# The normalised image turned between the two convolutions, and three steps beside it put later

## The reference

```python
x = x + L0(_gn(x))      # pixel similarity: s = relu(cos(p, q)) ** 2 over all pairs of pixels, y = s @ (W x + b)
x = x + L1(_gn(x))      # deformable convolution
# L1:
offset = conv2d_same(conv2d_same(x, w1, b1), w2, b2)     # 3x3, 128 -> 128 -> 72 channels
return relu(deform_conv(x, offset, wd))                  # 3x3, 4 groups: bilinear samples at shifted positions
```

## Time and profile before

| | |
|---|---|
| time, median of 3 runs | 460.2 us (459.57 to 460.83) |
| the profiled execution | 459.05 us, its span 457.0 us |
| busy: TensorE | 405.2 us (89%) |
| busy: VectorE, ScalarE, GpSimd | 339.5 us (74%), 215.6 us (47%), 90.0 us (20%) |
| mean granted TensorE clock | 0.970 |
| all DMA queues | 32.71 MB, mean 72 GB/s |
| stages 0, 1, 2, 3 (TensorE) | about 108 to 217, 217 to 319, 319 to 402, 402 to 457 us |

### The profile page before, as it was taken

How to read it: one execution, slowest core, us unless ns; L and a number is a source line. 1 busy time by engine, 2 the same in 40 slices (tenths; PEclk the granted TensorE clock), 3 DMA queues, 4 the chain that set the end, 5 groups by cost and what they waited for, 6 DMA issues and landing times.

```text
span 457.0 us, 9689 instructions
## 1 busy us (share of the span) xinstructions
PE 405.2 (89%) x3887; PEld 291.9 (64%) x3887; DVE 339.5 (74%) x586; ACT 215.6 (47%) x392; POOL 90.0 (20%) x99
## 2 busy tenths in 40 slices
PE   6698989979998789799999798989869898979996
PEld 6455557646665565678666575768556566857875
DVE  5995776829999999388854999376979945779901
ACT  3343254345555365441655446331845643257661
POOL 5444470001774100000546100000010000000000
PEclk9899999999999899999999899989979997999999
DMA  7200002250011124332001313442213243303330
GB/s 252 77 0 0 0 2 75 84 141 1 2 47 46 47 67 146 85 90 91 12 13 36 92 54 94 124 126 81 59 47 100 90 122 98 104 23 107 96 105 24
DMA packets 46157, 32.71 MB, mean 72 GB/s; under 512 B 3264, under 2 KB 43488, under 8 KB 46112
## 3 DMA queue, kind: packets, MB, share of 16 engines
q1 hardware_dynamic: 46048, 31.95, 23.5%
q10 hardware_dynamic: 64, 0.13, 0.1%
HBM read 25.24 MB, written 10.37 MB: 78 GB/s over the span
## 4 chain that ended last, share of the span: by engine, by line
PE 46%; DVE 32%; DMA 6%; SPq 5%; issue 4%; ACT 4%; POOL 1%; DVEq 0%; ACTq 0%; POOLq 0%
PE psB L788 10%; PE psB L555 9%; PE psT L739 7%; DVE wpix L1507 7%; PE psV L762 5%; DVE combo L1294 4%; PE psA L646 4%; DMA h_scr<-h_ring 3%; SPq L320 3%; DVE combo_p L1298 2%; DVE tent L1488 2%; PE psA L555 2%; DVE tent L1482 2%; PE psB L813 2%; PE psA L813 2%
## 5 line engine op out<-in xcount | busy, mean ns | idle before, releaser
L1021 ACT ACTIVATE wcell<-psT 128x512 f32<-128x512 f32 (+1 forms) x160 | 83.9, 552 | 70.2 <-PE psT L739 68.9
L1507 DVE TENSOR_TENSOR wpix<-tent 128x512 f32<-128x512 f32 (+1 forms) x160 | 99.7, 675 | 14.4 <-PE psT L739 13.3
L739 PE MATMUL psT<-ident,wpix 128*128 128x128 f32 x576 | 89.1, 288 | 12.4 <-ACT wcell L1021 12.0
L739 PEld LDWEIGHTS psT<-ident,wpix 128*128 128x128 f32 x576 | 68.8, 148 | 37.2 <-issue 29.5
L493 POOL TENSOR_TENSOR sim<-rel 128x512 f32<-128x512 f32 x48 | 61.4, 1299 | 69.0 <-ACT rel L978 69.0
L1045 ACT ACTIVATE val<-psV 128x576 f32<-128x576 f32 x64 | 44.0, 688 | 30.7 <-PE psV L762 30.2
L788 PE MATMUL psB<-val,wd_sb 128*128 128x256 f32 x216 | 51.2, 392 | 0.0
L762 PE MATMUL psV<-wcell,hwin 64*32 64x144 f32 x2048 | 47.2, 294 | 3.9 <-ACT val L1045 3.5
L646 PE MATMUL psA<-sim,scratch 128*128 128x512 f32 x96 | 45.6, 597 | 0.6 <-POOL sim L493 0.6
L788 PEld LDWEIGHTS psB<-val,wd_sb 128*128 128x128 f32 x216 | 40.7, 193 | 8.3 <-issue 2.9
L555 PE MATMUL psB<-g_p 128*128 128x512 f32 x144 | 40.9, 419 | 0.0
(11 more groups left out here) (193 smaller groups left out, 453.6 us busy)
## 6 DMA issues: line engine op xcount, KB each, us to landing
hwin<-h_scr SPq DMA_DIRECT2D x128, 128.0 KB, 2.9
h_scr<-h_ring SPq DMA_DIRECT2D x8, 576.0 KB
h_ring<-sim SPq DMA_DIRECT2D x4, 512.0 KB
x_all<-x SPq DMA_DIRECT2D x1, 1536.0 KB, 10.0
out<-yout SPq DMA_DIRECT2D x12, 128.0 KB, 1.8
off_scr<-sim SPq DMA_DIRECT2D x4, 288.0 KB
combo<-sim SPq DMA_DIRECT2D x32, 32.0 KB
val<-w SPq DMA_DIRECT2D x1, 576.0 KB, 6.1
```

What stands on the lines that cost most here:

```text
L739: last = pe.transpose(bank[:, at:at + P], wpix[:, t % 2, k, 2 * h:2 * h + 2, :].rearrange("p g q -> p (g q)"), ident[:, :])
L1021: act.activation(wcell[:, t % 2, taps[0]:taps[-1] + 1, :, :].rearrange("q k h p -> q (k h p)"), bank[:, 0:len(taps) * G // 2 * P], ACT.Cop ...
L1507: dve.tensor_tensor(w, ty, tx, ALU.mult).then_inc(s["weights_done"], 1)
```

## The change

In the steady stages the image is turned in slot 45 instead of 33, between the two convolutions. It now waits for conv1's output rows, and conv2 instead of conv1 waits for the copied image. On SyncE the store comes a tile later, ahead of the windows of tile 6, and the copy into windows ahead of those of tile 7, just ahead of the shifts. The offsets are turned in slots 67 and 69 instead of 65 and 67, with the first weights behind them in slot 69. The fourth batch's square moves from slot 56 to 57, its high and low parts from 58 to 60, the norms, gx and inversion from 61 to 62, add and scale from 62 to 63. The start before stage 0 keeps its slots.

```diff
-                      shift=None, turn={65: (0, 1), 67: (2, 3)}, extremes=70)
-        LEAD_IMAGE, STEADY_IMAGE, IMAGE_TILE = 38, 33, 5
+                      shift=None, turn={67: (0, 1), 69: (2, 3)}, extremes=70)
+        LEAD_IMAGE, STEADY_IMAGE, IMAGE_TILE = 38, 45, 6
...
-        PREP = {56: ("normalise", "square"), 58: ("high", "low"), 61: ("norms", "gx", "invert"), 62: ("add", "scale"),
+        PREP = {56: ("normalise",), 57: ("square",), 60: ("high", "low"), 62: ("norms", "gx", "invert"), 63: ("add", "scale"),
                 71: ("diagonal",)}
...
-        LEAD_WEIGHTS, FIRST_WEIGHTS, LEAD_EXTREMES = 60, 67, 12
+        LEAD_WEIGHTS, FIRST_WEIGHTS, LEAD_EXTREMES = 60, 69, 12
...
                     if t == IMAGE_TILE and b + 1 < B:
                         store_image(b + 1)
-                    if t == IMAGE_TILE + 1 and b + 1 < B:
+                    if t == ROWT - 1 and b + 1 < B:
                         lay_image(b + 1)
...
-                    if kx == 0 and which == 0 and v == 2:
+                    if kx == 0 and v == 2 and which == (1 if b else 0):
                         pe.wait_ge(s["image_copied"], 2 * (b + 1))
...
                 pe.wait_ge(s["flat_done"], b + 1)
                 if b > 0:
-                    pe.wait_ge(s["orelu_done"], 4 * (b - 1) + ORELU0)
-                if b + 1 < B:
-                    pe.wait_ge(s["rel_done"], 2 * QT * (b + 2 if b else 1))
+                    pe.wait_ge(s["conv1_done"], 2 * (b + 1))
+                else:
+                    pe.wait_ge(s["rel_done"], 2 * QT)
```

## The result

The changed kernel takes 464.97 us (median of 4 runs, 464.35 to 466.63) against 460.29 us (459.57 to 460.83) before: a ratio of 1.0108, with a 95% interval of 1.0078 to 1.0139. It is about 4.7 us slower; forecast was no change (460.0, range 456.5 to 463.0). The profiled execution of after took 464.68 us, its span 462.8 us against 457.0, at a mean clock of 0.958 against 0.970.

What follows compares the result with a forecast made beforehand. Chain of waits: TensorE 46%, VectorE 32%, transfers and SyncE's issuing 11%. Terms 0.6 - 3.5 + 2.4 + 0.3 = -0.2 us on 459.05 gave 458.85; with 1.15 us to the median, 460.0 us, range 456.5 to 463.0.

Steps and rivals of the forecast that it cites:

- the fourth batch's gain: Stage 0: ScalarE evicts psT ahead of the square, TensorE gets 2.30 us back; dconv 3.5 us earlier.
- slot 33's 0.2 us each: Image turn out of slot 33: 0 at full clock, 0.2 us each in stages 0, 1, 2 for the clock.
- the landing: Offsets' shifts land behind the copy on SyncE's queue, at 196.0, 301.8 and 383.1 us in stages 0 to 2.
- the stretch between landing and dconv: Offsets landed to dconv going on: 2.4 us in stage 0, 4.0 to 4.3 in stages 1 and 2.
- The two terms: Offsets' landing: 14.0 us for lay_image's copy on four engines, plus 1.7 us for nine shifts queued behind it.
- The halt at slot 60: Stage 0, TensorE waiting for an eviction of psT: down from 2.69 us to 0.4.
- the six matmuls: dconv behind the offsets' halt: 1.56 us at full clock, 2.93 at half; stage 1 may lose 0 to 1.4.
- Slot 45: Image turn into slot 45: 1.0 us of transposes hidden by a halt of 0.86; taken as 0, bounds 0 to 0.3.
- the later turn: Offsets' turn, stages 1 and 2: four transposes now come ahead of it, 0.35 us, twice that at half clock.
- Slower by the clock: Lengthened halts at slots 33 and 67 cost clock too: +3, 463 us; chance 0.28, including without stage 0's gain.
- The shifts don't queue: Stages 1 and 2 halt only 1.5 us at the offsets, -1 each, stage 0 -3.8: 455 us; chance 0.10.
- Faster, as the clock comes back soon: Offsets to dconv 2.4 us and matmuls at full clock in stages 1 and 2: about 457 us; chance 0.20.
- The fourth, that the change does nothing it says: Halt at slot 60 stays, stage 0 gives 0 to -1; ends in the slower case, chance 0.28.

Runs made afterwards that it cites:

- fill67: Changed kernel with 36 transposes of the identity, read by nobody, ahead of the wait for the offsets in stages 1 and 2: 460.25 us.
- copy12: Changed kernel with the copy into windows written rows first, spread over 12 transfer engines instead of 4: 453.56 us.
- image_undone: Changed kernel with the image turned in slot 33 again as before; the fourth batch and offsets keep their new slots: 451.91 us.
- fill33: Changed kernel with 32 transposes of the identity, read by nobody, in TensorE's halt of slot 33 in stages 0 and 1: 465.95 us.
- prep_undone: Changed kernel with the fourth batch's old slots: 467.34 us.
- copy12_fill33: Changed kernel with the copy on 12 engines and 32 unread transposes in the halt of slot 33 of stages 0 and 1: 452.67 us.
- image_only: Kernel before with the image's move alone; the fourth batch and the offsets in their old slots: 468.24 us.
- turn_undone: Changed kernel with the offsets turned in slots 65 and 67 again, the first weights in 67: 468.41 us.
- copy12_turn_undone: Changed kernel with the copy on 12 engines and the offsets turned in slots 65 and 67: 457.87 us.

## Why the prediction was wrong

**The mechanism was right, its sizes weren't.** The forecast had the fourth batch's gain spent on shifts that queue behind the copy. The runs show both. With slot 33's 0.2 us each, stages 0 to 3 were forecast at -3.3, +2.6, +0.5 and 0; they came out at -1.4, +4.3, +1.5 and +1.4.

The step that failed first is the landing: 14.0 us for the copy and 1.7 for the shifts. It took 0.9 to 1.7 us longer in each stage, 3.6 of the some 6 us that the sum was short of. The next is the stretch between landing and dconv in stages 1 and 2, which ran wholly at half clock behind the longer halts (4.59 us, where 4.0 to 4.3 were taken). The rest is mainly the 1.4 us of stage 3, of which the prediction has nothing; what slot 33 was off by in the three stages nearly cancels.

**When the offsets land.** The two terms gave 15.7 us from lay_image's issue to TensorE's turn. It took 16.7, 17.4 and 16.6 us (198.04 behind 181.34 in stage 0, 302.17 behind 284.73 in stage 1, 386.25 behind 369.69 in stage 2). That is 1.0 us more in stage 0, 1.7 in stage 1 and 0.9 in stage 2. The 14.0 us came from a copy that ran alone; here windows and shifts ran beside it. Which of the two terms was short is not shown.

**Stage 0.** The other 1.0 us of its miss came with slot 33: SyncE issued lay_image at 181.34 and not 180.3. Tile 6's windows ahead of it, which wait for a sample, went out 0.89 us later than in before, just as the sample of slot 38 came 0.89 us later. Then 2.5 us from the turn to dconv, reckoned as 2.4. The halt at slot 60 was as forecast (0.39).

**The clock behind the turn.** Between landing and dconv the forecast had 4.0 to 4.3 us in stages 1 and 2, from a row that was itself partly at half clock, and 0.5 of the possible 1.4 us for the six matmuls. Measured were 4.59 us and 1.85 for the matmuls in stage 1. The larger error here is what was not asked: that in the new slots this stretch runs in 2.5 us at full clock, so that the clock alone decides over 2 us in each stage. fill67, copy12 and image_undone each show 2.5. For stage 0 the prediction had summed up just that, 2.4 us; for stages 1 and 2 it took the old slots' row.

**Slot 33.** At full clock 0, as forecast (fill33: the sample waits for val again). For the clock 0.2 us was taken in each stage; stage 0 lost 1.0 at the sample, stage 1 about nothing (265.04 against 266.31, with the stage starting 1.37 earlier), and stage 2 gained 0.5 (350.01, with the stage starting 2.91 later, against 347.57). The bounds of stages 0 and 1 held, stage 2 fell below its 0, and the sum of +0.6 was near by luck: a loss of 1.0 and a gain of 0.5 met.

**Slot 45.** Free, as forecast: the image's turn has no halt ahead of it, and the halt of 0.86 us behind it is gone; the next one, at slot 51, is 0.71 us, and was 0.88.

**What was missed for the good.** In stages 1 and 2 the later turn was put at one group of transposes, 0.35 us, twice that at half clock; as a whole it is worth 2.5 to 4.3 us, as TensorE no longer waits for VectorE between the halves of the turn and, in some executions, as the clock stays up behind shorter halts. The fourth batch's slots were put at 2.30 us at the halt and gave 5.1 alone. The image's move was put at some 3 us and cost 13 in place of image_undone. The forecast of no change was the difference of gains and losses that were each put too small.

**The rivals.** "Slower by the clock" had the right sign and named the two turns, but put its price at the sample of slot 38. That point cost 1 us of the loss; the larger price was at the turns, where the rival had 1 us. "The shifts don't queue" fell to the halts of 5.25 and 4.36 us, and to copy12. "Faster, as the clock comes back soon" fell to the stretches at 0.50; but its 2.4 us from the offsets to dconv is what image_undone shows. The fourth, that the change does nothing it says, fell to the 0.39 us.

**Open.** Stage 3 lost another 1.4 us in the profiled execution of after. There the clock was low in a stretch where before has none:

```profile
409.85:413.26 3.41, 3.22 (x15) 2.55 (x14) 3.34 (x7) 1.71 (x4) 0.00 (x0) 0.50 0.00 0
```

The order of stage 3 was not changed, and this doesn't go with the image's move: at the same place prep_undone, fill67 and copy12_fill33 have a stretch at 0.50 too, while the other nine profiled executions, image_only, turn_undone and fill33 among them, stay at 1.00. What decides it is not shown. Nor is it shown that the shifts waited for the engines that they share with the copy, and not for the copy as such: in copy12 the copy was nearly over when they were issued, and no run has a slow copy on engines that the shifts don't use.

## What to carry to other kernels

When a slow transfer is moved on a queue, ask what is issued behind it within its own duration: 1152 KB on a quarter of the engines made small transfers behind it fly 4 us longer, and exchanging two dimensions of its pattern took that away. Price a halt of TensorE by its length and by the work behind it at either level of the clock: here the same stretch took 4.59 us at the lower level and 2.52 at full clock, behind a wait that ended no earlier. Look for the waits between the pieces of a step as well as ahead of it: by the estimate above, two waits for VectorE inside the turn were most of what its later slots gave. Cost the parts of a change apart, as a good part can hide a bad one: without the image's move this one is 1.8% faster than before.

## What was not expected of the hardware

- The lower clock level stayed through dense work: in 385.95 to 392.78 of after TensorE was busy for 6.53 of 6.83 us at 0.50.
- TensorE's clock is kept up by work that nobody reads: 36 transposes of the identity ahead of a wait that ended no earlier (302.25) took 2.07 us off the stretch behind it (4.59 to 2.52), with the granted clock at 1.00 there.
- Halts of nearly one length went both ways in one execution: 1.77 us, followed by a sample of 1.21 us, and 1.78 us, followed by one of 0.72 (copy12_turn_undone, stages 1 and 2).
- The last of nine transfers of 32 KB, in flight for 2.42 us in before, took 6.46 us behind a copy issued 11 us ahead of it on the same queue.
